# The last mixture stage of an eight-stage transformer kernel: dense experts replaced by gathered tokens

## What is computed

```
def _L3_ffn_ref(x, gate_query, log_temp, w1, b1, w2, b2):      # x: layer norm of the residual
    ...
    # logits [B, 16, 512] = gate_query . x / exp(log_temp)
    # six rounds: subtract logsumexp over the 16 experts, then over the 512 tokens
    # affinity = exp(t); each expert of each batch takes its CAP = 32 highest tokens
    # per expert: gelu(tokens @ w1 + b1) @ w2 + b2, times the affinity, added back to the tokens' places
```

## Time and profile before

| | us |
|---|---|
| runs | 4037.40, 4019.77, 4023.46; median 4023.46 |
| profiled execution, its own time | 4037.6 |
| its span in the trace | 4035.8 |
| last stage in it, from about 3690.7 to the end | 345 |
| PE busy, share of the span | 3219.9, 80% |
| DVE, ACT, POOL busy | 51%, 50%, 20% |
| mean granted TensorE clock | 0.901 |

### The profile page before, as it was taken

How to read it: one execution, slowest core, us unless ns; L and a number is a source line. 1 busy time by engine, 2 the same in 40 slices (tenths; PEclk the granted TensorE clock), 3 DMA queues, 4 the chain that set the end, 5 groups by cost and what they waited for, 6 DMA issues and landing times.

```text
span 4035.8 us, 50769 instructions
## 1 busy us (share of the span) xinstructions
PE 3219.9 (80%) x15467; PEld 1058.9 (26%) x15467; DVE 2039.0 (51%) x3495; ACT 2022.7 (50%) x2811; POOL 812.2 (20%) x1313
## 2 busy tenths in 40 slices
PE   6798999848787887878786268787878878885699
PEld 2243333212222222222222112222222222222243
DVE  3313444238374756566572656564737465653311
ACT  4442333317566565647473136474656656563344
POOL 0002444322222122222121122121221212220000
PEclk9898999869899899989898679898989989997799
DMA  1010000001111101010110010111111110100011
GB/s 37 12 35 21 1 1 1 9 18 36 30 38 34 33 24 46 23 41 25 34 36 24 0 38 25 31 34 34 36 31 34 32 39 25 45 22 22 18 35 35
DMA packets 125507, 110.57 MB, mean 27 GB/s; under 512 B 49902, under 2 KB 116028, under 8 KB 125244
## 3 DMA queue, kind: packets, MB, share of 16 engines
q1 hardware_dynamic: 114876, 97.84, 8.4%
q10 hardware_dynamic: 10368, 9.44, 0.8%
HBM read 41.95 MB, written 0.52 MB: 11 GB/s over the span
## 4 chain that ended last, share of the span: by engine, by line
PE 66%; DVE 15%; ACT 6%; issue 6%; POOL 3%; ACTq 1%; SPq 1%; DMA 1%; DVEq 0%; POOLq 0%
PE ps L507 10%; DVE arena L772 7%; PE ps L452 5%; PE ps L1161 4%; PE ps L1166 4%; PE ps L481 4%; PE ps L625 3%; PE ps L615 3%; PE ps L573 3%; PE ps L535 3%; PE ps L1431 2%; ACT arena L650 2%; PE ps L559 2%; PE ps L1447 2%; PE ps L524 2%
## 5 line engine op out<-in xcount | busy, mean ns | idle before, releaser
L650 ACT ACTIVATE arena<-ps 128x1024 f32<-128x1024 f32 x960 | 936.5, 1023 | 340.3 <-PE ps L481 336.6
L772 DVE TENSOR_REDUCE arena<-ps 128x1 f32<-128x512 f32 x1536 | 966.0, 684 | 216.6 <-PE ps L452 191.4
L507 PE MATMUL ps<-arena 128*32 128x512 f32 x3840 | 514.7, 610 | 20.5 <-ACT arena L650 18.0
L452 PE MATMUL ps<-arena 49*128 49x512 bf16 x1536 | 319.4, 412 | 240.5 <-DVE arena L772 201.1
L481 PE MATMUL ps<-arena 52*128 52x512 bf16 x1920 | 346.9, 388 | 28.4 <-ACT arena L650 25.0
L774 DVE TENSOR_REDUCE arena<-ps 128x3 f32<-128x462 f32 (+1 forms) x576 | 303.2, 579 | 108.0 <-PE ps L459 104.3
L852 POOL TENSOR_TENSOR arena<-arena,zeros 128x16 bf16<-128x16 f32 x192 | 42.6, 222 | 1084.2 <-DVE arena L772 643.5
L452 PEld LDWEIGHTS ps<-arena 49*128 49x128 bf16 x1536 | 75.3, 94 | 592.9 <-DVE arena L772 494.0
L862 POOL TENSOR_TENSOR arena<-arena 128x512 f32<-128x512 f32 x96 | 122.1, 1272 | 452.4 <-ACT arena L682 452.4
L868 POOL TENSOR_TENSOR arena<-arena 128x512 bf16<-128x512 f32 (+1 forms) x84 | 92.6, 1102 | 529.9 <-ACT arena L709 529.9
L792 DVE SCALAR_TENSOR_TENSOR tmp<-tmp,arena,rstd 128x512 f32<-128x512 f32 x72 | 54.1, 752 | 270.8 <-ACT rstd L699 268.5
(11 more groups left out here) (318 smaller groups left out, 4504.3 us busy)
## 6 DMA issues: line engine op xcount, KB each, us to landing
arena<-arena SPq DMA_DIRECT2D x720, 64.0 KB
arena<-we_dram SPq DMA_DIRECT2D x24, 578.5 KB, 3.7
arena<-arena ACTq DMA_DIRECT2D x144, 64.0 KB
w<-weights_dram SPq DMA_DIRECT2D x26, 320.0 KB, 3.0
w<-weights_dram SPq DMA_DIRECT2D x13, 512.0 KB, 3.7
arena<-arena SPq DMA_DIRECT2D x384, 6.0 KB
arena<-arena SPq DMA_DIRECT2D x288, 19.2 KB
w<-weights_dram SPq DMA_DIRECT2D x39, 128.0 KB, 2.2
```

Of the source, the lines that this page charges most:

```text
L452: pe.matmul(s_bank(slot + r), qst[b][rows, idx, P * qt:P * (qt + 1)], kst[b][rows, idx, :], start=True, stop=True).then_inc(s_full, 1 + (z ...
L507: mm = pe.matmul(bank(7)[32 * j:32 * j + 32, :], v, prob[:, slot, j, :], start=(g % 2 == 0 and kt == 0), stop=(a == 0 and g % 2 == 1 and k ...
L650: act.activation(prob[:, chunk_no(b, a, g, kt) % NPROB, 2 * p:2 * p + 2, :], e_bank(slot).rearrange("p (j n) -> p j n", j=2), ACT.Exp, sca ...
L772: op = ve.tensor_reduce(nmax[:, g % 2, r, n:n + 1], s_bank(slot + r), AX.X, ALU.max, negate=True)
```

## The change

Only the last stage is changed; `moe_*` stay as they were for the second stage but for the bias that only the last one used.

- **Both batches at once.** `te`, `pick7`, `junk7` hold 64 partitions (batch 0's experts on 0 to 15, batch 1's on 32 to 47) by 512 tokens in place of 16 by 1024. The opening scales 64x512 once; a round has 4 transposes each way, one maximum, one exponential, one correction; the selection has four steps in all. In the first three rounds PE and ACT also turn `xn` to tokens on partitions (`xnT7`) and make the slot numbers 1 to 32.
- **Ranks and one-hot matrices.** PE turns the gates to tokens on partitions. DVE marks the chosen (`selT7`); PE multiplies by a triangle of ones (made by POOL at the stage's start) to number each expert's chosen tokens; `hot` compares numbers and slots, for each batch and block of 128 tokens and 8 experts (16 instructions of 128x256). POOL multiplies them by the gates (`gated7`, 8 instructions of 128x512).
- **Gather.** 16 matmuls of 256 columns pick 32 tokens for each expert and batch; DVE copies them to `chosen7`.
- **Experts.** Each expert works on 64 columns (32 tokens, 2 batches): 4 matmuls of 64 columns for the hidden layer, ACT's gelu with bias in 4 instructions of 128x64, 4 matmuls for the output, DVE adds the bias (128x64). Written out, not as a loop; `hidden(e+1)` stands ahead of `outs(e)`.
- **Putting back.** Between the experts PE turns the gated one-hot blocks (8 times 4 transposes) and four experts' outputs (4 times 2 transposes), DVE copies both out of PSUM, and PE multiplies them (4 times 2 matmuls of 512 columns), adding up in PSUM. DVE adds that to `x`.
- **Loads.** SP issues four small loads, after POOL has cleared their places, and then all 16 experts' weights one after the other.

```
@@ b7_pe @@
-            for r in range(ROUNDS):
-                ...
-                for t in range(TT):
-                    tr = pe.transpose(bank(2)[:, E7 * t:E7 * (t + 1)], te[0:E7, P * t:P * (t + 1)], ident[0:E7, 0:E7])
-                ...
-            moe_pe(pe, c, 7)
+            def hidden(e):
+                pe.wait_ge(w_pair2[e // 2], pairs_held + 32)
+                pe.wait_ge(s7["chosen"], B * (e // 8 + 1))
+                ...
+                for t in range(FT):
+                    mm = pe.matmul(bank(e % 2)[:, 64 * t:64 * (t + 1)], wexp7[:, e, P * t:P * (t + 1)],
+                                   chosen7[:, e], start=True, stop=True)
+                mm.then_inc(s7["hid_mm"], 1)
+            ...
+            def scatter(g):
+                for b in range(B):
+                    pe.wait_ge(s7["ring_out"], 1 + max(RING7.index(("back", g, b)), RING7.index(("eo", g))))
+                    pe.matmul(bank(4 + b), eoT7[:, g, b, :], back7[:, g, b, :], start=(g == 0), stop=(g == KS - 1))\
+                      .then_inc(s7["back"], 1)
+            ...
+            for half in range(2):
+                ...
+                for b in range(B):
+                    pe.wait_ge(s7["turned"], b + 1)
+                    for t in range(KS):
+                        pe.wait_ge(s7["hot"], B * KS * half + KS * b + t + 1)
+                        mm = pe.matmul(bank(4 + 2 * half + b)[:, 0:SLOTS7 // 2], xnT7[:, b, t, :], hot7[:, b, t, part], start=(t == 0),
+                                       stop=(t == KS - 1))
+                    mm.then_inc(s7["gathered"], 1)
+            hidden(0)
+            for e in range(E7):
+                if e + 1 < E7:
+                    hidden(e + 1)
+                if 0 <= e - 2 < KS * B:
+                    turn_back((e - 2) // B, (e - 2) % B)
+                outs(e)
+                if e and e % 4 == 0:
+                    turn_outs(e // 4 - 1)
+                if e > 4 and e % 4 == 1:
+                    scatter(e // 4 - 1)
+            turn_outs(KS - 1)
+            scatter(KS - 1)
@@ b7_dve @@
+            for b in range(B):
+                for t in range(KS):
+                    hot(0, b, t)
+            for t in range(KS):
+                hot(1, 0, t)
+            for b in range(B):
+                chosen(0, b)
+            for t in range(KS):
+                hot(1, 1, t)
+            for b in range(B):
+                chosen(1, b)
@@ b7_pool @@
+            gp.wait_ge(s7["dve_step"], DVE7 + 11)
+            for b in range(B):
+                for t in range(KS):
+                    ...
+                    gp.wait_ge(s7["hot"], B * KS + KS * b + t + 1)
+                    gp.tensor_tensor(blocks(gated7[:, b, t, :]), blocks(hot7[:, b, t, :]),
+                                     gateT7[:, at:at + E7].unsqueeze(2).broadcast_to([P, E7, CAPACITY]), ALU.mult)\
+                      .then_inc(s7["gated"], 1)
@@ b7_sp @@
-            moe_sp(sp, c, 7)
+            sp.wait_ge(s7["cleared"], 2)
+            ...
+            for e in range(E7):
+                sp.dma_start(wexp7[:, e], dram["we3"][P * e:P * (e + 1), :]).then_inc(w_pair2[e // 2], 16)
```

More of the change, by code:

```diff
@@ L1806, in build @@
         at5 = dict(zip(TIMES5, spent3))
-        spent5 = [a + (list(TIMES5.values())[i] if i < len(TIMES5) and FIRST <= 5 <= LAST else 0)
-                  for i, a in enumerate(spent3)]
         def b5_pe(pe, c):
@@ L1918, in b5_sp @@
             sp.dma_start(wq5[:, 2 * FI * P:], dram["wd5"]).then_inc(s5["loaded"], 16)
[L1921 removed]
+        used[0] = 0
         E7, ROUNDS, CAPACITY = 16, 6, 32
[L1923 removed]
+        ROWS7 = 64
+        SLOTS7 = E7 * CAPACITY
+        wexp7 = carve(E7 * MOE_COLS).rearrange("p (e n) -> p e n", e=E7)
+        gq7 = carve(ROWS7)
         temp7 = carve(8)
         coef7 = carve(8)
[L1926 to L1929 removed]
@@ L1935, in build @@
-        s7 = dict(zip(EVENTS7, events))
-        at7 = dict(zip(EVENTS7, spent5))
-        def b7_pe(pe, c):
+        tri7 = [carve(3 * P // 2) for _ in range(2)]
+        ones7 = carve(P)
+        slot_no7 = carve(CAPACITY)
+        xnT7 = carve(T).rearrange("p (b t n) -> p b t n", b=B, t=KS)
+        hot7, gated7 = (carve(B * KS * SLOTS7).rearrange("p (b t n) -> p b t n", b=B, t=KS) for _ in range(2))
+        back7 = carve(KS * B * S).rearrange("p (g b n) -> p g b n", g=KS, b=B)
+        hid7 = carve(2 * FT * B * CAPACITY).rearrange("p (r t n) -> p r t n", r=2, t=FT)
@@ new lines, in build @@
+        chosen7 = h[:, :].rearrange("p (e b c) -> p e b c", e=E7, b=B)
+        eo7 = tmp[:, :].rearrange("p (b n) -> p b n", b=B)
+        eoT7 = lg[:, :].rearrange("p (g b n) -> p g b n", g=KS, b=B)
+        s7 = {k: sem("choice_" + k) for k in (
+            "cleared", "loaded", "step", "pe_step", "act_step", "dve_step", "turn_mm", "turned", "hot", "gated", "gathered",
+            "chosen", "hid_mm", "hid", "out_mm", "eo", "ring_mm", "ring_out", "back")}
+        PE7, ACT7, DVE7 = 2 + 2 * ROUNDS, 1 + 4 * ROUNDS, 1 + 7 * ROUNDS
@@ new lines, in b7_pe @@
+                if r < B:
+                    for t in range(KS):
+                        tr = pe.transpose(bank(6 + r)[:, P * t:P * (t + 1)], xn[:, r * S + P * t:r * S + P * (t + 1)], ident)
+                    tr.then_inc(s7["turn_mm"], 1)
+                elif r == B:
+                    pe.wait_ge(s7["cleared"], 6)
+                    pe.wait_ge(s7["step"], 8)
+                    pe.matmul(bank(3)[:, 0:CAPACITY], ones7, tri7[1][:, tri_at:tri_at + CAPACITY], start=True, stop=True)\
+                      .then_inc(s7["turn_mm"], 1)
@@ new lines, in b7_pe @@
+            pe.wait_ge(s7["turned"], 3)
+            pe.wait_ge(s7["dve_step"], DVE7 + 10)
+            tile = B * E7
+            pe.matmul(bank(3)[:, 0:KS * tile], tri7[1][:, tri_at:tri_at + P], selT7, start=True, stop=False)
+            for t in range(KS - 1):
+                mm = pe.matmul(bank(3)[:, tile * (t + 1):KS * tile], ones7, selT7[:, 0:tile * (KS - 1 - t)], start=False,
+                               stop=(t == KS - 2))
+            mm.then_inc(s7["pe_step"], 1)
+            for half in range(2):
+                part = slice(SLOTS7 // 2 * half, SLOTS7 // 2 * (half + 1))
+                for b in range(B):
+                    pe.wait_ge(s7["turned"], b + 1)
+                    for t in range(KS):
+                        pe.wait_ge(s7["hot"], B * KS * half + KS * b + t + 1)
+                        mm = pe.matmul(bank(4 + 2 * half + b)[:, 0:SLOTS7 // 2], xnT7[:, b, t, :], hot7[:, b, t, part], start=(t == 0),
+                                       stop=(t == KS - 1))
+                    mm.then_inc(s7["gathered"], 1)
@@ new lines, in b7_act @@
+            act.activation(junk7[0:ROWS7, :], te[0:ROWS7, :], ACT.Exp).then_inc(s7["act_step"], 1)
+            act.preload_act_table_set("gelu_apprx_tanh_and_others")
+            for e in range(E7):
+                if e >= 2:
+                    act.wait_ge(s7["out_mm"], e - 1)
+                act.wait_ge(s7["hid_mm"], e + 1)
+                for t in range(FT):
+                    at = 2 * DFF + P + t
+                    act.activation(hid7[:, e % 2, t, :], bank(e % 2)[:, 64 * t:64 * (t + 1)], ACT.Gelu_apprx_tanh,
+                                   bias=wexp7[:, e, at:at + 1]).then_inc(s7["hid"], 1)
```

285 lines of the change are left out of this document (188 added, 97 removed).

## The result

The changed kernel took **3800.85 us** in the median of four runs (3800.29 to 3806.9), the kernel before 4023.82 in as many (4019.77 to 4037.4): a ratio of 0.9442, 95% interval 0.9429 to 0.9455, and 223 us less. It lies where the rival "full clock for the experts" put it, 3802: the range held because it reached out to that rival, while the course of the clock that the forecast itself took for the experts didn't come about.

The account below looks back on a forecast made before the run. PE alone bounds the mixture, a chain of small steps the balancing and selection. First comparison at 3752.1, plus gather 16, experts 58 and 2.55 behind: 207 us off the median 4023.46, giving 3816 us, range 3793 to 3840.

Parts of the forecast that it names:

- full clock for the experts: Rival for the experts: PE at full clock throughout, experts 43.4 us, gather 10 to 16; 3802 or 3795 us; chance 0.30.
- the course of the clock that the forecast itself took for the experts: Experts: half clock until the first putting back (after expert 5), full clock after it; 58 us; forecast chance 0.42.
- Opening, rounds, selection: Steps before the first comparison: opening +0.1, six rounds -16.3, selection -4.8 us, so that comparison starts at 3752.1.
- The price of a small matmul: PE's 128-column and the experts' 64-column records: 0.11 us each at full clock, 0.21 at half; fewer columns no cheaper.
- the 8-column row: Evidence from the earlier profile: 12 PE records of 8 columns took 2.10 us at half clock, PEld busy throughout.
- the columns' rival: Rival for the experts: moving columns alone set the pace, 14 us less than the full-clock case; 3785 us; chance 0.03.
- The gather: From the first comparison to the last gather matmul: 16 us, or 9.8 if undisturbed by POOL.
- comparison 10 and later take turns with POOL: up to six meetings of 1.1: In the gather, DVE's comparisons and POOL's gating exclude each other on the SBUF port pair: at most +6.6 us.
- the experts start at half: PE, sparse at the gather's end, begins the experts at clock 0.50; 29.4 us to the end of the first putting back.
- The rival by the weights: Rival for the loads: instructions or weights late, last pair landing at 3786, some 5 us; 3821 us; chance 0.07.
- the one by 27 GB/s: Rival for the loads: 16 queued weight loads stream at 27 GB/s, taking 343 us; 4032 us, slower than before; chance 0.01.
- half to the end: Rival for the experts: half clock throughout, 16 + 76 + 4 = 96 us, 22 more; 3838 us; chance 0.17.

## Why the prediction came out as it did

**What bounds the kernel; the sum's main term.** Right. PE alone bound the mixture and balancing added a chain of small steps; in the changed kernel the first comparison stands 19.5 us earlier after `x` than the mixture did, for the forecast's 21.0, and balancing and selection alone shortened the stage by 20.2.

**Opening, rounds, selection.** Right to 1.4 us in 60.9. The opening came out +0.4 for +0.1, a round 6.47 for 6.24, the selection from its exponential to the first comparison 10.9 for 10.7. The step that was short is "to tokens: 4: -0.4; to experts: 4: -0.9": half the transposes don't take half the time (0.69 for 1.03, 1.06 for 1.87), since a rest that doesn't depend on their number stays. That is 0.15 of the 0.23 in a round; most of the remainder is the correction with its copy, 0.72 less for 0.8.

**The price of a small matmul.** Right: 0.11 at full clock, 0.21 at half (eight follow one another by 0.89 and 1.71), and no cheaper for 64 columns than for 128. That it was taken from the 8-column row is what kept the forecast from the 3785 of the columns' rival. By columns alone, a 64-column record would take 0.054 at the pace of this trace's 512 (0.43), half of what it took. The Trainium skill's gap by moving columns ("TensorE: Matmul & The Clock Gate", Back-to-back issue gap), which it says undercounts small matmuls, does so here: 64 and 128 columns take the same 0.11. By the formula in that section of the Trainium skill a 64-column matmul would take 0.029, and 256 records would take some 21 us less (an estimate); the 14 in the prediction go by the pace of this trace.

**The gather.** Too long by 4.55 us. The undisturbed gather, 9.8, whose parts the prediction doesn't give, was 9.0 with POOL held back. "0.42 each" was 0.34, and "comparison 10 and later take turns with POOL: up to six meetings of 1.1" was four, of 0.85 each (4.84 for four in place of 1.42). Comparisons 10 to 12 were in a row that POOL's first gating didn't break. Holding POOL back gave 2.4 us in the stage, making the row unbroken 2.2. That DVE and POOL hinder each other is shown by both, and by POOL's first instruction, 1.0 alone, 1.77 beside the end of a row and 3.11 beside a longer one; who goes first is read from these three orders of the work, not tested further. The Trainium skill ("SBUF — State Buffer", SBUF: two separate sides) says that the port pair is locked for a whole instruction; the trace agrees for the last four (1.2 each against 0.36 alone), and the row of sixteen at 0.34 shows that POOL doesn't get it between two instructions that follow at once.

**The experts.** The step that failed: "with the comparisons waiting for POOL, PE is sparse at the end of the gather, so I take it that the experts start at half." PE was sparse there, 1.93 of 3.3 us, but the clock had risen in the dense first part and was not taken away before the experts. It makes 14.0 of the 17.2 us by which the stage was shorter than forecast. The rest of the term was nearly right: full clock 43.4 for 44.0 measured; half to the first putting back 58 for 58.0 in the kernel with the pause; 29.4 to the rise for 29.8. That the two totals agree so well is luck in part: both measured times hold 1.7 us for a last putting back at half clock, which the forecast had at full, so its other terms were 1 to 2 us too long. The clock did rise behind the first putting back when it was down, and small matmuls before it had not raised it, as the 8-column row had suggested. The profile of before held a hint in one place, a rise after 8.0 us of dense work at 3773; the gather's 256-column records are dense work of the same kind, and I had costed their time at both clocks but not asked what they do to the clock.

**Loads.** No cost, right, with a wrong size: 59 us at the rate of one load; 16 queued took 25.4 us, so the margin was larger. The rival by the weights and the one by 27 GB/s fall: no PE wait in the experts names a load. The 5 us of the first don't follow from its own numbers either: with the last pair landing at 3786, and the last two experts wanted near 3815 at the forecast's pace, it would have cost nothing.

**The rivals' chances.** "Full clock for the experts" had 0.30 and "half to the end" 0.17. Had I asked what the dense first part of the gather does to the clock, full clock would have stood ahead of the forecast's own course with its 0.42.

**The end.** 2.55 for 2.46. The last putting back at half clock costs 1.74; the forecast had it at full.

## What to carry to other kernels

Where the work shrinks so far that PE runs many small matmuls, cost them by the record and not by columns, and ask of the work right before them what it leaves the clock at: here it was worth 14 us in 44, and a pause of PE of 6.8 us behind the gather took them away. When an engine's own wait at a stage's opening names a small load, look whether the work behind it in the same queue needs that load; moving one ACT instruction gave 5.0 us. And where two engines hinder each other on one memory, as VectorE and GpSimd did here, it is cheaper to let each do its row at once: the row that paused for a copy met the other engine at each of its last four instructions.

## What the runs showed of the hardware that I had not expected

- The level of the clock hung on what had come before: 64-column float32 matmuls and 128-column transposes stayed at 0.50 for 25.5 us although PE never paused, and rose only behind four 512-column records; the same matmuls began at 1.00 in the changed kernel and stayed there, 13.6 us before the first putting back and 39 us with three of them in between.
- A row of 16 DVE instructions kept its pace of 0.34 us while POOL began work on the same memory, and POOL's first instruction stood for 3.11 in place of 1.0; four that came while POOL had work in hand took 1.2 each.
- Sixteen queued loads of 578.5 KB moved at 364 GB/s over 25.4 us; one of before's, from issue to landing, at 156.
- Streaming twice the columns through a small float32 matmul cost nothing that can be seen in eight records (1.06 both). The clock was still up in the last putting back in all four traces with 128 columns, and down in six of the seven with 64; the seventh, with the pause of PE ahead of the experts, also had it up (1.98). So that the columns did it isn't shown.
